# Three token tiles of the last combine summed on TensorE through diagonal coefficient matrices

## What is computed

```python
x = L0_attn_x
x = x + _L0_attn_ref(_layernorm(x, axis=-1), W_K, W_Q, W_V, W_O)
x = x + _L0_ffn_ref(_layernorm(x, axis=-1), router_weight, bias, gate, up, down, ...)
# inside _L0_ffn_ref
topk_idx, topk_w = _route(x, router_weight, e_score_correction_bias)
coeff = jnp.zeros((T, E), x.dtype).at[jnp.arange(T)[:, None], topk_idx].add(topk_w)
def body(acc, ws):
    g, u, d, c = ws
    h = jax.nn.silu(x @ g.T) * (x @ u.T)
    return (acc + c[:, None] * (h @ d.T), None)
out, _ = jax.lax.scan(body, jnp.zeros_like(x), (gate_proj, up_proj, down_proj, coeff.T))
shared = jax.nn.silu(x @ shared_gate.T) * (x @ shared_up.T) @ shared_down.T
return (out + shared).reshape(B, S, Hd)
```

## Time and profile before

| | |
|---|---|
| median of 3 runs | 1389.67 us (1386.99 to 1390.35) |
| the profiled execution's own time | 1384.97 us |
| its span, first to last instruction recorded | 1383.2 us |
| busy: PE, DVE, ACT, POOL | 95%, 66%, 53%, 42% |
| first of batch 1's additions on DVE | 1347.26 us |
| last of batch 1's additions on DVE | 1379.68 us |

### The profile page before, as it was taken

How to read it: one execution, slowest core, us unless ns; L and a number is a source line. 1 busy time by engine, 2 the same in 40 slices (tenths; PEclk the granted TensorE clock), 3 DMA queues, 4 the chain that set the end, 5 groups by cost and what they waited for, 6 DMA issues and landing times.

```text
span 1383.2 us, 28521 instructions
## 1 busy us (share of the span) xinstructions
PE 1307.6 (95%) x8530; PEld 1163.4 (84%) x8530; DVE 917.7 (66%) x1896; ACT 728.3 (53%) x1664; POOL 579.0 (42%) x587
## 2 busy tenths in 40 slices
PE   5999999999999899999989999999989998989994
PEld 4888888988889797888778888888878997889993
DVE  5666666666666968677886666666767742346638
ACT  2555555555555555454545555555535664556651
POOL 5535535254330404032135446353000764656576
PEclk9999999999999999999999999999999999999997
DMA  3252645525352000000001111011146998999983
GB/s 120 84 176 86 198 141 173 174 83 194 120 190 95 28 5 28 5 27 19 14 20 66 42 61 62 29 46 57 62 128 212 390 397 329 330 374 393 392 257 97
DMA packets 128821, 197.27 MB, mean 143 GB/s; under 512 B 10464, under 2 KB 100064, under 8 KB 128736
## 3 DMA queue, kind: packets, MB, share of 16 engines
q1 hardware_dynamic: 65328, 111.35, 23.8%
q10 hardware_dynamic: 51120, 51.26, 10.8%
q0 software_dynamic: 12288, 33.57, 6.8%
HBM read 109.10 MB, written 87.03 MB: 142 GB/s over the span
## 4 chain that ended last, share of the span: by engine, by line
PE 83%; DVE 8%; DMA 5%; ACT 2%; issue 2%; SPq 1%; ACTq 0%; POOL 0%; DVEq 0%
PE ps_s L763 9%; PE ps_t L822 8%; PE ps_s L765 8%; PE ps_s L764 8%; PE ps_x L763 6%; PE ps_x L764 6%; PE ps_x L765 6%; PE ps_z L763 5%; PE ps_z L765 5%; PE ps_z L764 5%; DMA ring_down<-experts_dram 4%; PE ps_t L988 3%; PE ps_z L988 3%; PE ps_s L957 2%; PE ps_t L763 2%; PE ps_t L764 2%
## 5 line engine op out<-in xcount | busy, mean ns | idle before, releaser
L1085 ACT ACTIVATE prob<-ps_s,neg_max 128x128 f32<-128x128 f32 (+7 forms) x256 | 189.6, 742 | 249.8 <-DVE neg_max L1273 248.5
L1288 DVE TENSOR_TENSOR pT_lo<-ps_t,pT_hi 128x512 fp32r<-128x512 f32 (+2 forms) x320 | 189.6, 604 | 105.0 <-ACT pT_hi L1101 101.3
L1101 ACT ACTIVATE pT_hi<-ps_t 128x512 fp32r<-128x512 f32 (+2 forms) x320 | 161.5, 533 | 95.2 <-PE ps_t L822 95.0
L1273 DVE TENSOR_REDUCE neg_max<-ps_s 128x1 f32<-128x128 f32 (+7 forms) x256 | 186.7, 749 | 8.3 <-PE ps_s L765 7.1
L661 POOL DMA_INDIRECT xs<-xn,slots x128 | 128.5, 1004 | 126.3 <-PE ps_z L988 61.3
L822 PE MATMUL ps_t<-ident,prob 128*128 128x128 f32 x1152 | 170.6, 273 | 7.7 <-DVE pT_lo L1288 3.6
L822 PEld LDWEIGHTS ps_t<-ident,prob 128*128 128x128 f32 x1152 | 137.0, 140 | 30.5 <-DVE pT_lo L1288 5.7
L763 PE MATMUL ps_s<-k_hi,q_hi 128*128 128x512 f32 (+2 forms) x384 | 154.8, 403 | 0.0
L763 PE MATMUL ps_s<-ring,a_hi 128*128 x384 | 126.5, 330 | 13.2 <-SPq L498 6.7
L576 POOL TENSOR_TENSOR a_hi<-raw_a,zero 128x512 fp32r<-128x512 f32 x32 | 33.3, 1042 | 243.5 <-PE ps_x L765 158.3
L765 PE MATMUL ps_s<-k_hi,q_lo 128*128 128x512 f32 (+2 forms) x384 | 133.7, 348 | 0.0
(11 more groups left out here) (275 smaller groups left out, 3666.2 us busy)
## 6 DMA issues: line engine op xcount, KB each, us to landing
ring<-ws SPq DMA_DIRECT2D x60, 512.0 KB, 5.8
xs<-taken SPq DMA_DIRECT2D x16, 1536.0 KB, 9.7
xq<-xs ACTq DMA_DIRECT2D x48, 512.0 KB
xs<-yq ACTq DMA_DIRECT2D x48, 512.0 KB, 9.2
ws<-split_to SPq DMA_DIRECT2D x34, 512.0 KB, 3.0
raw<-experts_dram SPq DMA_DIRECT2D x34, 256.0 KB, 3.4
raw_a<-w_a_dram SPq DMA_DIRECT2D x15, 512.0 KB, 4.2
ring_down<-experts_dram SPq DMA_DIRECT2D x60, 128.0 KB, 6.7
```

Of the source, the lines that this page charges most:

```text
L1085: act.activation(prob[c][:, j, 0:width(r)], ps_s[r % 2][:, 0:width(r)], ACT.Exp, bias=neg_max[:, r:r + 1], accum_out=row_sum[:, c, j:j + 1 ...
L1101: act.activation(to, ps_t[m % 2][:, j * P:], ACT.Copy).then_inc(s_hi, 1)
L1273: dve.tensor_reduce(neg_max[:, r:r + 1], ps_s[r % 2][:, 0:width(r)], AX.X, ALU.max, negate=True).then_inc(s_max, 1)
L1288: dve.tensor_tensor(lo, ps_t[m % 2][:, j * P:], hi.bitcast(F32), ALU.subtract).then_inc(s_bank_free, 1)
```

## The change

`tail_items` changes for batch 1. The additions of tiles 0 to 4 (five for each k, item "F", still on DVE) begin at step 103 instead of 104, stand ahead of the step's own items instead of behind them, and come five to a step for eight steps (103 to 110). Tiles 5 to 7 become item "D": three for each k, at steps 104 to 111, behind the step's own items. For each "D", ACT makes a 128 x 128 diagonal matrix of the coefficients (a copy of the identity scaled per row, into one of eight buffers that lie in `xq[0]`), and PE multiplies it with the gathered block, summing over the eight k in PSUM. Three items "S" at the end of the list add each sum to `acc` on DVE. The store of the last two routed tasks moves from the "B" of task 105 to just behind ACT's copy of task 103. SP's counts for the output follow the new order. POOL's gathers, their order and their waits are not touched.

```diff
--- before.py
+++ after.py
@@ -100,6 +100,10 @@
 TASKS = [("s", 0, NT), ("m", 0, PT), ("m", 1, PT), ("s", 1, NT)]
 TAIL = 36
 COMBINE = NT + PT + 6
+LAST_ROUTED = NT + B * PT - 1
+BY_DVE = 5
+BY_PE = NT - BY_DVE
+ADDS = NT * TOPK + BY_DVE * TOPK
 YQ, XQ, GATHERS = 4, 4, 64
 SCATTER_FROM, GATHER_FROM = 15, 15 + NT * TOPK // 2
 
@@ -144,15 +148,17 @@
 def tail_items():
 
 
-    result, late = [], [("F", 1, i) for i in range(NT * TOPK)]
+    result, late = [], [("F", 1, k * NT + t) for k in range(TOPK) for t in range(BY_DVE)]
     for n in range(TAIL, NTASK):
+        if n >= LAST_ROUTED:
+            result += late[:BY_DVE]
+            del late[:BY_DVE]
         result += step_items(n)
         if n >= COMBINE and 2 * (n - COMBINE) < NT * TOPK:
             result += [("F", 0, 2 * (n - COMBINE)), ("F", 0, 2 * (n - COMBINE) + 1)]
-        if n >= NT + B * PT:
-            result += late[:8]
-            del late[:8]
-    return result + late
+        if n > LAST_ROUTED:
+            result += [("D", t, n - LAST_ROUTED - 1) for t in range(BY_DVE, NT)]
+    return result + late + [("S", t, 0) for t in range(BY_DVE, NT)]
 
 
 def woven(order, extra):
@@ -367,6 +373,7 @@
     hT = [sb(f"hT{n}", [P, 2 * I])[:, :] for n in range(2)]
     yq = [sb(f"yq{n}", [P, 4 * D])[:, :] for n in range(YQ)]
 
+    diagonal = xq[0].rearrange("p a (h i) -> p (a h) i", i=P)
     rooms = [[r[:, :] for r in room_b0], [r[:, :] for r in room_b1]]
     rank_parts = [[rooms[b][1][:, n * NQ:(n + 1) * NQ].rearrange("p (t g h) -> p t g h", g=G, h=G)
                    for n in range(2)] for b in range(B)]
@@ -386,6 +393,7 @@
     ps_gu = [ps_s[n][:, 0:NQ] for n in range(2)]
     ps_xT = [ps_s[n][:, NQ:] for n in range(2)]
     ps_hT = ps_t[0][:, 0:D]
+    ps_sum = [bank[:, 0:D] for bank in (*ps_xT, ps_x)]
     ps_y = [ps_t[1][:, :], ps_z[:, :]]
 
 
@@ -414,6 +422,7 @@
     s_y, s_y_out, s_y_add = sem("y"), sem("y_out"), sem("y_add")
     s_ys = [sem(f"ys{n}") for n in range(YQ)]
     s_yg, s_acc = [sem(f"yg{n}") for n in range(GATHERS)], sem("acc")
+    s_diagonal, s_sum = sem("diagonal"), sem("sum")
     s_need = sem("need")
     s_out = [sem(f"out{b}") for b in range(B)]
 
@@ -544,8 +553,8 @@
         for n in range(B * NT // 2):
 
             b, t = divmod(2 * n, NT)
-            done = NT * TOPK - NT + t + 2
-            sp.wait_ge(s_acc, b * NT * TOPK + done)
+            sp.wait_ge(s_acc, (NT * TOPK - NT + t + 2) if b == 0 else
+                       ADDS - BY_DVE + t + 2 if t + 2 <= BY_DVE else ADDS + t + 2 - BY_DVE)
             sp.dma_start(out[b, t * P:(t + 2) * P, :].rearrange("(t p) d -> p t d", p=P),
                          acc[:, 2 * n:2 * n + 2, :]).then_inc(s_out[b], 16)
         for b in range(B):
@@ -1049,8 +1058,21 @@
 
         each_pair(pe, pair)
 
-        for kind, g, _ in tail_items():
-            moe(kind, g)
+        def add_gathered(t, k):
+
+            j, i = k * BY_PE + t - BY_DVE, NT * TOPK + k * NT + t
+            if j == 0:
+                pe.wait_ge(s_xs_lo, B * PT)
+            pe.wait_ge(s_diagonal, j + 1)
+            pe.wait_ge(s_yg[i % GATHERS], 16 * (i // GATHERS) + 16)
+            pe.matmul(ps_sum[t - BY_DVE], diagonal[:, j % 8, :], yg[i % GATHERS], start=k == 0,
+                      stop=k == TOPK - 1).then_inc(s_sum, 1)
+
+        for kind, g, k in tail_items():
+            if kind == "D":
+                add_gathered(g, k)
+            else:
+                moe(kind, g)
 
     @block.scalar
     def _(act):
@@ -1143,7 +1165,7 @@
                 if g >= 2:
                     act.wait_ge(s_y, 2 * g - 2)
                 act.activation(hT[g % 2], ps_hT, ACT.Copy).then_inc(s_hT_out, 1)
-                if 3 <= u <= B * PT + 1 and u % 2:
+                if 3 <= u < B * PT and u % 2:
                     store_rows(u // 2 - 1)
             elif kind == "C" and what == "m":
                 act.wait_ge(s_y, 2 * g + 2)
@@ -1152,6 +1174,8 @@
                     act.wait_ge(s_ys[q % YQ], YS0 + 16 * (q // YQ))
                 act.activation(yq[q % YQ][:, u % 2 * NQ:(u % 2 + 1) * NQ], ps_y[g % 2],
                                ACT.Copy).then_inc(s_y_out, 1)
+                if g == LAST_ROUTED:
+                    store_rows(u // 2)
             elif kind == "E":
                 act.wait_ge(s_xT, u + 1)
                 act.wait_ge(s_gu, g - 1)
@@ -1197,8 +1221,14 @@
 
         each_pair(act, pair)
 
-        for kind, g, _ in tail_items():
-            if kind != "F":
+        for kind, g, k in tail_items():
+            if kind == "D":
+                j = k * BY_PE + g - BY_DVE
+                if j >= 8:
+                    act.wait_ge(s_sum, j - 7)
+                act.activation(diagonal[:, j % 8, :], ident[:, :], ACT.Copy,
+                               scale=ck[1][:, g, k:k + 1]).then_inc(s_diagonal, 1)
+            elif kind not in "FS":
                 moe(kind, g)
 
     @block.vector
@@ -1502,7 +1532,7 @@
             t, k = gathered(i)
             at = b * NT * TOPK + i
             dve.wait_ge(s_yg[at % GATHERS], 16 * (at // GATHERS) + 16)
-            last_write(b, t, s_acc, at + 1)
+            last_write(b, t, s_acc, at + 1 if b == 0 else NT * TOPK + k * BY_DVE + t + 1)
             to = acc[:, b * NT + t, :]
             dve.scalar_tensor_tensor(to, yg[at % GATHERS], ck[b][:, t, k:k + 1], to,
                                      ALU.mult, ALU.add).then_inc(s_acc, 1)
@@ -1571,7 +1601,12 @@
         for kind, k, n in tail_items():
             if kind == "F":
                 combine(k, n)
-            else:
+            elif kind == "S":
+                dve.wait_ge(s_sum, BY_PE * (TOPK - 1) + k - BY_DVE + 1)
+                last_write(1, k, s_acc, ADDS + k - BY_DVE + 1)
+                to = acc[:, NT + k, :]
+                dve.tensor_tensor(to, ps_sum[k - BY_DVE], to, ALU.add).then_inc(s_acc, 1)
+            elif kind != "D":
                 moe(kind, k)
```

## The result

| | before | after |
|---|---|---|
| median, 7 runs each | 1388.18 us | 1384.06 us |
| ratio, 95% interval | | 0.9971 (0.9959 to 0.9983) |
| the profiled execution's own time | 1384.97 us | 1383.94 us |
| its span | 1383.22 us | 1382.16 us |
| start of "down" of task 104 in it | 1345.66 us | 1348.73 us |

What follows compares the result with a forecast made beforehand. POOL's last gather issue, delayed by DVE's addition chains, was taken to bound the end: 5.2 us from that issue and 0.3 from landing, less 1.0 for the matmul, 4.6 us sooner; 1389.67 - 4.5 = 1385.2 us, range 1382.8 to 1388.4.

Steps and rivals of the forecast that it cites:

- POOL's last issue: Start of gather 63: from 1375.6 to 1370.4, giving 5.2 us of the 4.6 us gain.
- PE's step: PE from one "down" to the next: 2.51 + 1.30 for three matmuls = 3.81 us, plus 0.1 for diagonals.
- POOL behind a task: POOL's gathers that wait for a "down": start 0.27 us behind its end, gather 62 at 1368.4.
- Held gathers at the end: Gathers 60 and 61 beside the k = 7 additions: 60 delayed 0.2, 61 held until the third or fourth addition.
- the window named: Start of gather 63: 1369.7 with nothing held, 1371.7 with 60 held for the whole chain; 1370.4 taken.
- The end: Behind the last gather: landing 3.8 us, matmul 1.0, "S" addition 0.4, output 3.0; span ends at 1378.6.
- The clock: PE's last matmul, after standing some 3 us: 1.0 us at the lower clock level, 0.6 at full clock.
- Costing nothing: Step 103's five additions fit DVE's 2.09 us of idling; the store, 1.2 us sooner, brings and costs nothing.
- nothing held: Rival: chains of five let every gather through; gather 63 at 1369.7, gain 5.3 to 5.9 us, 1384.0; chance 0.17.
- POOL not freed: Rival: something other than additions stretches the gathers; last issue stays at 1375.6, 1387.7 to 1390.6 us; chance 0.15.
- full holding: Rival: gathers asking during a chain wait for its end; gather 63 at 1371.7, gain 3.3 us, 1386.4; chance 0.12.
- the clock: Rival: PE's clock falls inside steps 105 to 110, slow steps 7.6 us; from three on 1396.6 us; chance 0.05.

Runs made afterwards that it cites:

- the first experiment: Kernel before, second input of batch 1's 64 additions from PSUM instead of SBUF: from "down" of task 104 to the end 33.56 us, against 37.56.
- the last experiment: Changed kernel, last gathers behind "down" of 106, one wait less per gather from 24, diagonals a step ahead, six tiles DVE, two PE; rerun: 1378.66 us, ratio 0.9946.

## Why the prediction was right, step by step

The forecast was 4.5 us sooner, and 4.1 were measured. The mechanism was right: chains of additions with two SBUF inputs held the gathers, POOL's last issue was what came late, and with the chains cut short the last gathers follow PE's tasks. The rule of the Trainium skill ("SBUF — State Buffer", "Who interferes with whom"), that a VectorE instruction with two SBUF inputs contends with a GpSimd instruction that reads SBUF, is borne out by the first experiment. That each such instruction locks the other side out for its whole length does not describe the rows here, in two ways. The gather of 1351.51 in the changed kernel, begun in the middle of a chain of five, and the late ones of the last experiment run undisturbed beside additions. And held gathers waited for more than one addition: that of 3.20 us sat through six, 0.40 us apart, to the end of the chain. Which gathers are held goes with where in the chain they begin (before, those begun in the sixth of eight took 2.07 us each time, those in the second 1.15); the rows give no rule for it. How long a chain of five would hold a gather was therefore a guess.

The sizes were less good than their sum, and that the sum came so close is partly luck: POOL's last issue came 4.1 us sooner instead of 5.2, and the 0.6 us that the forecast took off behind it were not lost.

- *PE's step.* Forecast 3.81 us, with 0.1 for the diagonals; measured 4.02. The first diagonal is ready 0.93 us after "down" starts, as worked out, but the wait also lengthens the first matmul's own spacing. Over six steps this is 1.3 us at "down" of 110. It is the top of my bound (1.2), and I had argued that it would lie beside the time for which gathers are held. It did not, since they no longer were.
- *POOL behind a task.* Forecast 0.27 us, measured 0.78. The row that I took is of batch 0, whose gathers take one wait less. The trace of before had the other value: "down" at 1274.56 for 1.03 us, the gather behind it at 1276.38.
- *Held gathers at the end.* Forecast 0.7 us for gathers 60 and 61; measured none. The issue of the last gather came at 25.79 us of the tail, against 24.74 forecast: 1.3 + 0.5 - 0.7. In the forecast's times that is 1371.5, inside the window named (1369.7 to 1371.7), but it lies late in it because of PE's steps and POOL's second wait, and not because of the holding that set the window's upper end.
- *The end.* Here a step of the reasoning failed. I had the last gather's landing, a matmul, an addition and 3.0 us of output on the path. None of them is. In both kernels the span ends 7.63 us after the last gather's start: POOL's own closing instruction (a DRAIN in the trace) ends 6.46 us after that gather's end, and the others wait for it. SP, which waits for the output, was through 0.4 us sooner in the kernel before and 1.0 us sooner in the changed one; the last gather landed after 2.75 us, not 3.8, and it made no difference. So the 1.0 us that I charged for the matmul, and the 0.3 that I gained by the landing, do not count. By the right rule my own last issue, 24.74, gives a tail of 32.4 and a gain of 5.2 us; the delays of 1.3 and 0.5 us, less the 0.7 of holding, bring it to 4.1.
- *The clock.* The last matmuls ran at full rate (two records in 0.67 us), with 1.00 granted up to 1375, where the kernel before had 0.53 from 1367 on.
- *Costing nothing*, as forecast: the five additions at step 103, the moved store, DVE's load.

The rivals: nothing held was nearest to the truth about the gathers; POOL not freed, full holding and the clock did not occur in the changed kernel's trace. The clock did fall to its lower level inside the steps of the changed kernel's variants on other chips, but behind standstills of PE of 2 to 4 us and not behind the short waits for diagonals. The ratio, 0.29% of gain, fell on the line between faster and no change, where the forecast had put nearly even chances.

## What to carry to other kernels

Before costing what lies behind the last transfer, ask which engine closes the program last: an indirect DMA issued late on GpSimd moves the end by its own issue time, whatever is done with its data. Where GpSimd issues indirect DMAs beside long runs of VectorE instructions with two SBUF inputs, cut the runs or take one input from PSUM. When one hold is removed, look at once for the next wait in line, and take its latency from a row with the same number of waits.

## What the runs showed of the hardware

- A back-to-back chain of additions with two SBUF inputs can withhold something from a gather until the chain's end: held gathers ended 0.82 to 0.83 us behind it, so by an estimate (0.95 - 0.82) they ask for it about 0.13 us after their start. A chain of eight held one for 3.20 us, a chain of five one for 1.95. With one input from PSUM, 18 of 18 gathers took 0.94 to 0.95 us.
- POOL's closing instruction ended 6.46 us after the end of its last indirect DMA in all thirteen traces of kernels without an additional gather and 6.54 in the one with it. Where it is the last to finish, the span ends 7.63 us after that DMA's start.
- A second wait that has long been met, in front of an indirect DMA on POOL, adds 0.5 us to its start behind the one that is met last (0.78 against 0.27).
- Chips differ: the kernel before took 1388 us on some and 1417 to 1424 on others, where ACT shows pauses that nothing in the trace releases, most of them of 3 to 4 us, the longest of 10.8 us.
- PE's clock can fall inside a step: behind a pause of PE of 2 to 4 us on those chips it was granted 0.50 and 0.54 over the next 6 to 7 us, and four records took 2.05 us instead of 1.03.
